# Two heads' last contexts rounded from the transposed banks, the picks behind the first projection, remainders last

## The reference

```python
def _cross_attention(q_in, kv_in, wq, bq, wk, bk, wv, bv, wo, bo, bias_k, bias_v):
    qh = (q_in @ wq + bq).reshape(b, q_len, H, K)
    kh = (kv_in @ wk + bk).reshape(b, t, H, K)
    vh = (kv_in @ wv + bv).reshape(b, t, H, K)
    kh = concatenate([kh, broadcast(bias_k)], axis=1)
    vh = concatenate([vh, broadcast(bias_v)], axis=1)
    weights = softmax(einsum('bqhk,bthk->bhqt', qh, kh) / sqrt(K))
    return einsum('bhqt,bthk->bqhk', weights, vh).reshape(b, q_len, H * K) @ wo + bo

x = x + _cross_attention(layer_norm(x, ln1), xf, ...)
x = x + _cross_attention(layer_norm(x, ln2), xf, ...)
x = x + gelu(layer_norm(x, ln_mlp) @ w_fc1 + b_fc1) @ w_fc2 + b_fc2
```

## Time and profile before

| what | us |
|---|---|
| three runs, median (lowest to highest) | 1197.35 (1195.98 to 1198.78) |
| profiled execution, whole | 1196.6 |
| its span, first to last instruction | 1194.8 |
| PE busy | 1182.8 |
| POOL busy | 873.6 |
| DVE busy | 892.3 |
| ACT busy | 763.6 |
| granted TensorE clock, mean | 0.999 |

### The profile page before, as it was taken

One profiled execution on the slowest core, in us unless ns is written; L12 is line 12 of the kernel. 1 busy time (PEld: TensorE's weight loads), 2 busy tenths in 40 slices (PEclk: granted clock), 3 DMA queues, 4 the chain that ended last, 5 costly groups with the idle time before them and its releaser, 6 DMA issues.

```text
span 1194.8 us, 26508 instructions
## 1 busy us (share of the span) xinstructions
PE 1182.8 (99%) x7688; PEld 1103.5 (92%) x7688; DVE 892.3 (75%) x1584; ACT 763.6 (64%) x1501; POOL 873.6 (73%) x744
## 2 busy tenths in 40 slices
PE   8999999999999999999999999999999999999999
PEld 7889999999999999998998999999999999999898
DVE  6978877787878786777776977777777777777854
ACT  5756666666666666676585666666666666667765
POOL 4848878787878788677552879696969696967763
PEclk9999999999999999999999999999999999999999
DMA  5411232222222222233230122222222222222331
GB/s 159 146 30 52 59 77 58 76 58 76 58 76 59 74 60 74 51 70 100 89 97 19 40 60 74 62 73 61 73 62 73 60 74 60 75 49 69 78 95 43
DMA packets 148297, 83.61 MB, mean 70 GB/s; under 512 B 121180, under 2 KB 122604, under 8 KB 148248
## 3 DMA queue, kind: packets, MB, share of 16 engines
q1 hardware_dynamic: 147704, 82.27, 26.7%
q10 hardware_dynamic: 544, 0.75, 0.2%
HBM read 68.56 MB, written 0.53 MB: 58 GB/s over the span
## 4 chain that ended last, share of the span: by engine, by line
PE 92%; DVE 2%; issue 2%; DMA 2%; ACT 1%; POOL 1%; POOLq 0%; SPq 0%; DVEq 0%; ACTq 0%
PE psum L803 38%; PE psum L810 13%; PE psum L816 13%; PE psum L811 13%; PE psum L768 5%; PE psum L856 4%; PE psum L782 2%; DMA w_raw<-weights 1%; PE psum L716 1%; PE psum L732 1%; DVE oth L1548 0%; DVE t_max L1417 0%; PE psum L837 0%; ACT oth L1174 0%; POOL ctx L563 0%
## 5 line engine op out<-in xcount | busy, mean ns | idle before, releaser
L628 POOL TENSOR_TENSOR pt<-slots,pt 125x512 fp32r<-125x512 f32 (+3 forms) x384 | 453.5, 1188 | 159.2 <-ACT slots L1099 153.7
L803 PE MATMUL psum<-qs,ctx 128*125 128x384 f32 (+1 forms) x2304 | 527.5, 367 | 1.2 <-DVE qs L1385 0.8
L803 PEld LDWEIGHTS psum<-qs,ctx 128*125 128x125 f32 x2304 | 397.1, 186 | 42.4 <-issue 1.9
L810 PE MATMUL psum<-ctx,pt 125*128 125x258 f32 (+1 forms) x1344 | 378.2, 283 | 0.7 <-ACT on L1106 0.6
L811 PE MATMUL psum<-ctx,pt 125*128 125x256 f32 (+1 forms) x1344 | 376.9, 282 | 0.0
L816 PE MATMUL psum<-ctx,pt 125*128 125x258 f32 (+1 forms) x1344 | 369.3, 282 | 0.0
L1096 ACT ACTIVATE pt<-slots 125x512 fp32r<-125x512 f32 (+3 forms) x384 | 221.2, 576 | 219.2 <-DVE slots L1401 213.9
L1417 DVE TENSOR_TENSOR t_max<-psum,t_max 125x512 f32<-125x512 f32 (+1 forms) x282 | 175.2, 621 | 156.8 <-PE psum L803 154.8
L810 PEld LDWEIGHTS psum<-ctx,pt 125*128 125x128 f32 (+1 forms) x1344 | 253.5, 189 | 12.0 <-issue 1.5
L811 PEld LDWEIGHTS psum<-ctx,pt 125*128 125x128 f32 (+1 forms) x1344 | 254.2, 189 | 6.5
L816 PEld LDWEIGHTS psum<-ctx,pt 125*128 125x128 f32 (+1 forms) x1344 | 250.5, 190 | 0.3 <-POOL pt L628 0.2
(11 more groups left out here) (108 smaller groups left out, 1029.7 us busy)
## 6 DMA issues: line engine op xcount, KB each, us to landing
nat_stage<-ctx_nat SPq DMA_DIRECT2D x60, 375.0 KB
tr_stage<-ctx_tr SPq DMA_DIRECT2D x60, 375.0 KB, 3.1
w_raw<-weights SPq DMA_DIRECT2D x70, 256.0 KB, 2.7
qt<-turn SPq DMA_DIRECT2D x256, 32.0 KB, 2.0
qt<-turn SPq DMA_DIRECT2D x224, 24.0 KB, 1.9
dk_rest<-dk_rows SPq DMA_DIRECT2D x6, 256.0 KB, 3.8
w_raw<-weights ACTq DMA_DIRECT2D x2, 256.0 KB, 4.8
dk_first<-dk_rows SPq DMA_DIRECT2D x2, 256.0 KB, 4.3
```

What stands on the lines that cost most here:

```text
L628: nc.gpsimd.tensor_tensor(split_weights(h, LO, c), logits(h, c), as_f32(split_weights(h, HI, c)), ALU.subtract).then_inc(pt_lo, 1)
L803: last = mm(scores(h, k, first), ctx_tr_chunk(half, a, c), qs[h][:, m, half, 0:R], start=(half, a, m) == terms[0], stop=(half, a, m) == te ...
L810: mm(out_bank[:, 0:D + 2], hi, ctx_nat_hi(c), start=(c == 0), stop=False, skip_group_check=True)
```

## The change

Three things. First, `project` makes the terms of a context projection in another order: high x high, then weights' low x contexts' high, then weights' high x contexts' low. Queries and the MLP keep the old order. Second, TensorE makes the picks between head 0's and head 1's projection instead of ahead of both. Third, heads 0 and 1 take the last batch's contexts from three places: the first half (4 tiles) from `qt` as before, tiles 0 and 1 of the last half from bank 7 and tile 2 from bank 1, without the way through `qt`. The copies to `qt` stay, for the other heads, but come later: ScalarE's behind both remainders (`oth_lo`), VectorE's behind its subtractions, and its copy to `pn_extra` behind that.

```diff
+        def turned_heads(s):
+            return OT_BANK[:, 0:DC * 2 * P].rearrange("p (c n r) -> p c n r", c=DC, r=P)[:, :, :, s * TQ:(s + 1) * TQ]
+        def last_turned_heads(s):
+            return OT_LAST[:, 0:DC * P].rearrange("p (c r) -> p c r", c=DC)[:, :, s * TQ:(s + 1) * TQ]
...
-                for a, m in TERMS:
+                order = TERMS if ready is None else (TERMS[0], TERMS[2], TERMS[1])
+                for a, m in order:
...
-            def first_contexts(n, job):
+            def first_contexts(n, job, picks):
                 for u in range(2):
                     pe.wait_ge(c_lo, INIT + n + u - 3)
                     project(C_BANK[u][:, 0:ROWS], u, job + u, lambda m, c, u=u: oth[u][:, m, c, :],
                             ((oth_hi, INIT + n + u + 1), (oth_lo, INIT + n + u + 1)), True).then_inc(oth_used, 1)
+                    if u == 0:
+                        picks()
...
 ACT
                 normalized(B - 1, 1, O_LAST)
+                act.wait_ge(moved, INIT + (l + 1) * (TURNED * MOVES * 16))
+                turned_at = late.start + GT[0]
+                for s in range(2):
+                    go(by_tile(oth[s][:, HI])[:, :, late.start:turned_at], head_rows_of(s)[:, :, late.start:turned_at],
+                       ACT.Copy).then_inc(oth_late, 1)
                 act.wait_ge(ot_mm, INIT + l * 2 + 1)
+                for s in range(2):
+                    go(by_tile(oth[s][:, HI])[:, :, turned_at:turned_at + 2], turned_heads(s), ACT.Copy)
+                    if s == 0:
+                        act.wait_ge(ot_mm, INIT + l * 2 + 2)
+                    go(by_tile(oth[s][:, HI])[:, :, late.stop - 1], last_turned_heads(s), ACT.Copy).then_inc(oth_hi, 1)
+                act.wait_ge(oth_lo, INIT + l * H + 2)
                 last_at = (batch_at(l, B - 1) + 1) * TILES
                 go(qt_tiles[:, :, last_at - GT[1]:last_at - 1], OT_BANK ..., ACT.Copy).then_inc(ot_out, 1)
                 act.wait_ge(ot_out, INIT + l + 1)
                 act.wait_ge(ot_last, INIT + l + 1)
-                act.wait_ge(moved, INIT + (l + 1) * (TURNED * MOVES * 16))
-                for s in range(2):
-                    go(by_tile(oth[s][:, HI])[:, :, late], head_rows_of(s)[:, :, late],
-                       ACT.Copy).then_inc(oth_hi, 1)
...
 DVE
                 normalized(B - 1, 1, O_LAST)
+                for s in range(2):
+                    dve.wait_ge(oth_late, INIT + l * 2 + s + 1)
+                    V.tensor_tensor(LO of oth[s], first half's 4 tiles, from qt, ALU.subtract)
+                dve.wait_ge(oth_hi, INIT + l * H + 2)
+                for s in range(2):
+                    V.tensor_tensor(LO of oth[s], 2 tiles, from turned_heads(s), ALU.subtract)
+                    V.tensor_tensor(LO of oth[s], last tile, from last_turned_heads(s), ALU.subtract).then_inc(oth_lo, 1)
+                V.tensor_copy(qt[... last tile], OT_LAST ...).then_inc(ot_last, 1)
                 extra_weights(B - 1, 1)
-                dve.wait_ge(ot_mm, INIT + (l + 1) * 2)
-                V.tensor_copy(qt[... last tile], OT_LAST ...).then_inc(ot_last, 1)
-                for s in range(2):
-                    dve.wait_ge(oth_hi, INIT + l * H + s + 1)
-                    V.tensor_tensor(LO of oth[s], all 7 tiles, from qt, ALU.subtract).then_inc(oth_lo, 1)
```

More of the change, by code:

```diff
@@ L259, in build @@
         dvm_ready, oth_early, oth_hi, oth_lo = sem("dvm_ready"), sem("oth_early"), sem("oth_hi"), sem("oth_lo")
+        oth_late = sem("oth_late")
         oth_used = sem("oth_used")
@@ L275, in build @@
             "act": [saved, xn_act, w_hi, h_hi, q_hi, qp_out, most_qs_hi, first_qs_hi, copied, exp_hi, exp_done, on_act, ot_out,
-                    p80_hi, oth_early, oth_hi, c_hi, g32_ready],
+                    p80_hi, oth_early, oth_late, oth_hi, c_hi, g32_ready],
             "dve": [filled, x_ready, ln_stats, ln_aggr, ln_chain, xn_dve, h32_ready, h_lo, dk_ready, cq_step, cq_ready,
@@ L768, in project @@
                         last = mm(out_bank, w[u][:, a, c * P:(c + 1) * P], moving(m, c),
-                                  start=(a, m, c) == (HI, HI, 0), stop=(not more and (a, m, c) == (LO, HI, DC - 1)))
+                                  start=(a, m, c) == (HI, HI, 0), stop=(not more and (a, m, c) == (*order[-1], DC - 1)))
                 return last
@@ L988, in _, with picks @@
                 context_transposes(2, GT[1], OT_LAST)
[L990 to L996, removed]
+                def picks():
+                    pe.wait_ge(consts_in, 16 * N_CONSTS)
+                    pe.wait_ge(pn_ready, INIT + (l + 1) * GROUPS)
+                    settle(pe)
+                    for j in range(TQ):
+                        last = mm(PICK_BANK[0:EXTRA, j * NT:(j + 1) * NT], pick[:, j, :], pn_extra[:],
+                                  start=(j == 0), stop=True, skip_group_check=True)
+                    last.then_inc(pn_picked, 1)
                 heads, jobs = l * H, l * JOBS + H
-                first_contexts(heads, jobs)
+                first_contexts(heads, jobs, picks)
                 output_quad(heads, jobs, True, True, False)
@@ L1537, in _ @@
                 normalized(B - 1, 1, O_LAST)
-                extra_weights(B - 1, 1)
-                dve.wait_ge(ot_mm, INIT + (l + 1) * 2)
-                V.tensor_copy(qt[:, (batch_at(l, B - 1) + 1) * TILES - 1], OT_LAST[:, 0:DC * P].rearrange("p (c r) -> p c r", c=DC)).then_inc(ot_last, 1)
-                for s in range(2):
-                    dve.wait_ge(oth_hi, INIT + l * H + s + 1)
-                    V.tensor_tensor(by_tile(oth[s][:, LO])[:, :, late], head_rows_of(s)[:, :, late],
-                                    by_tile(as_f32(oth[s][:, HI]))[:, :, late], ALU.subtract).then_inc(oth_lo, 1)
+                turned_at = late.start + GT[0]
+                for s in range(2):
+                    dve.wait_ge(oth_late, INIT + l * 2 + s + 1)
+                    V.tensor_tensor(by_tile(oth[s][:, LO])[:, :, late.start:turned_at], head_rows_of(s)[:, :, late.start:turned_at],
+                                    by_tile(as_f32(oth[s][:, HI]))[:, :, late.start:turned_at], ALU.subtract)
+                dve.wait_ge(oth_hi, INIT + l * H + 2)
+                for s in range(2):
+                    V.tensor_tensor(by_tile(oth[s][:, LO])[:, :, turned_at:turned_at + 2], turned_heads(s),
+                                    by_tile(as_f32(oth[s][:, HI]))[:, :, turned_at:turned_at + 2], ALU.subtract)
+                    V.tensor_tensor(by_tile(oth[s][:, LO])[:, :, late.stop - 1], last_turned_heads(s),
+                                    by_tile(as_f32(oth[s][:, HI]))[:, :, late.stop - 1], ALU.subtract).then_inc(oth_lo, 1)
+                V.tensor_copy(qt[:, (batch_at(l, B - 1) + 1) * TILES - 1], OT_LAST[:, 0:DC * P].rearrange("p (c r) -> p c r", c=DC)).then_inc(ot_last, 1)
+                extra_weights(B - 1, 1)
                 def context_lo(h, s):
```

## The result

The changed kernel takes 1208.54 us, median of 4 runs (1207.09 to 1209.06), against 1197.33 before: 1.009 of the time before, 95% interval 1.0079 to 1.0102. It is slower by 11 us, far outside the range given (1196.5 to 1203.2). The forecast was wrong.

A forecast was written before the change was run, and what follows sets the result against it. TensorE, busy 99%, was taken as the bound, with time to win only in pauses where attention hands over to the output projection. Per junction +0.88 - 0.31 + 0.2 = +0.77, twice +1.5, gave 1198.9 us; range 1196.5 to 1203.2.

The forecast's parts named there:

- The likeliest case: Attention-to-output-projection junctions: pn_extra copy waits out the second weight remainder; +0.77 per junction, +1.5 in the run; 42%.
- The pn_extra copy meets the second weight remainder ... and is done at 542.4: VectorE, first junction: the last copy waits for GpSimd until about 542.3; picks start 0.10 behind it.
- my upper bound: First junction: a 64-element subtraction misses its turn, the copy waits to 544.5, head 2's contexts end at 549.1, +3.0.
- rival 3: The picks, waiting on the pn_extra copy, miss GpSimd's gap: +5.8, 1203.2, or +4.2, 1201.5, if only the copy is late; 25%.
- the one case of L1548: VectorE operation at 543.27 before the change that got its turn between two otherwise back-to-back weight remainders; basis for the middle case.
- rival 2: TensorE's clock falls to 1.2 GHz behind the pauses: one junction +3.2, 1200.6; both +4.9, 1202.3; 25%.
- The bound of +3.0 per junction: Most the wait for pn_extra costs by the end of head 2's contexts, if a 64-element subtraction misses its turn.
- Up to +9: Whole run, 1206, if the picks miss GpSimd's gap and the clock falls too; left outside the range.
- Head 0's start: TensorE, without the picks to fill it, pauses from 539.50 to 540.2 between the transposes and head 0's projection.
- Remainders last: Context projections need the contexts' remainder 0.43 later: -0.31 at head 4, +0.2 at head 5 for an earlier-needed weight remainder.
- The gain is 0.1: ScalarE rounding from the banks: head 0's high part ready at about 540.2 instead of 540.3, head 1's 540.45 instead of 540.5.
- Most to win is 2.3: All TensorE pauses at the junctions: about 1.15 per junction, 2.3 in the run, 0.19%.

The follow-up runs named there:

- b1: Changed kernel with TensorE products of zeros filling its two pauses, 4 and 4 in the first layer, 1 and 12 in the second: 1203.97 us, 1.0054 of before.
- d3: Changed kernel with the late copy to pn_extra written as a maximum of the value with itself, two SBUF inputs instead of one: 1207.43 us, 1.0088 of before.
- e1: Changed kernel with VectorE's two last copies swapped, pn_extra before the last tile, and head 1 waiting for ot_last: 1205.07 us, 1.0064 of before.
- a1: Changed kernel with the copy to pn_extra back right behind the normalising, and head 1's projection waiting for ot_last: 1200.17 us, 1.0022 of before.
- a4: Changed kernel, but GpSimd makes the weight remainders of heads 2 and 3 only after the copy to pn_extra: 1200.43 us, 1.0032 of before.
- a2: Kernel before with only the new order of a context projection's terms: 1196.84 us, 0.9994 of before.
- c1: Kernel before with the new order of terms and GpSimd's mask product ahead of the weight remainder: 1196.23 us, 0.9989 of before.
- b2: Kernel before with only the roundings and subtractions from the banks, head 1 waiting for ot_last: 1199.66 us, 1.0021 of before.
- d2: c1 with the last half's pn_extra values made from the banks, one operand from PSUM and one from SBUF: 1196.35 us, 0.9991 of before.
- b3: Kernel before with the picks behind head 0's projection and the pn_extra copy behind the two subtractions, last tile's copy ahead: 1200.24 us, 1.0026 of before.

## Why the prediction was wrong

The order in which I put the cases was wrong, more than their mechanisms. The likeliest case (+1.5) had the copy done 2.9 us behind the transposes. It was 4.61 and 5.15.

- **"The pn_extra copy meets the second weight remainder ... and is done at 542.4"**: the step that failed. In the first layer the first 64-element subtraction waited out all four mask products, where I had it run behind the second, and the next missed its turn by 0.05 as in my upper bound (TensorE took up head 0's remainder 2.99 behind the transposes, where I took 2.0). The copy was asked for beside the third weight remainder, and without the clock (b1) F came 2.94 later, the +3.0 of rival 3. In the second layer the subtractions came sooner than I took (1.79), the copy did meet the second remainder, and then it waited for the two behind it too. I had it get its turn at the first switch, by the one case of L1548; b1, d3 and e1 show the other outcome again. So rival 3, which I gave 25%, is what happened, with rival 2 on top.
- **The bound of +3.0 per junction** was too low: F came 4.06 and 6.06 later. It left the clock out (1.12 and 2.55 by b1); for the waits alone it was right in the first layer (2.94) and short in the second (3.51), where the copy let two switches pass.
- **The clock (rival 2)** fell in both junctions. b1 puts it at 3.7 by F and 4.6 by the medians, where the rival had 3.4 for both: the price was about right. I named it as an alternative to rival 3; here the two came together, and with the copy back in its place (a1) or the pauses filled (b1) the profiled executions kept the clock. "Up to +9" was the nearest I came, and I put it outside the range.
- **Head 0's start** was right in the first layer: TensorE paused 0.83 ahead of it (0.7 forecast). It was 0.37 in the second, and 0.41 and 0.51 in the first junction of b1 and a4; it moves with the landing of the last moves.
- **Remainders last**: head 4's 0.31 went as forecast, F gained 0.4 by it (a2). But head 5 lost 0.6, not 0.2: the mask product that met VectorE. In c1, without that meeting, it loses the 0.2.
- **"The gain is 0.1"** for the rounding from the banks alone: b2 has +2.6 for that part. I followed it to head 0 and not to head 2.
- **Most to win is 2.3** held: the best kernel has about 1.1 of it.

By parts: the order about -0.5, the picks' place +2.3, the banks +2.6, each measured alone; the changed kernel has 11.2. The rest, about 7, is what the parts do together: a copy of 3 elements that comes late enough to meet GpSimd's run, and TensorE with nothing left to do and its clock falling.

## What to carry to other kernels

In these traces a tiny VectorE operation with all its data in SBUF cost what GpSimd had in hand when it was asked for, 0.15 to 3.32 us. So place it by GpSimd's order and not by its own length, or let it read one operand from PSUM (0.16 in d2). Before moving filler work (here the picks) off a waiting engine, count the pauses on both sides as one, and price the clock with them. And where a wait shortened releases another engine earlier, look at what that engine then collides with.

## What the runs showed of the hardware

- Small VectorE operations from SBUF beside GpSimd: 0.15 to 0.16 us with GpSimd idle (a4, b3); 1.24 in all three cases (changed kernel, b1, d3) when asked for 0.05 behind the start of the first of two gapless weight remainders; 2.98 to 3.32 in all five cases (changed kernel, b1, d3, e1 twice) when asked for during the first of three. That they let one switch pass and then another I had not expected. The Trainium skill, SBUF — State Buffer, "SBUF: two separate sides", says that the one that starts first has the ports for its whole operation; the traces agree, and show more: in the five cases the waiting VectorE did not get them between GpSimd's operations either. Why it got its turn at the first switch in the three cases and only behind the last in the five stays open.
- Reading one operand from PSUM took it out of the contention: 0.16 in both layers (d2), beside a weight remainder that held the copy for 1.27.
- In the changed kernel's first junction the clock fell to 0.50 at about 546.05, behind pauses of 0.83, 1.12 and 1.04 us with 1.04 and 0.68 of matmuls between and 1.1 behind the last, and stayed there for 3.4 us, in which TensorE was always busy; in the second it fell at the end of a pause of 2.79 and stayed for 6.8. In a1, with pauses of 0.96 and 0.99, it stayed at 1.00 in the profiled execution.
